# The experts of the second half and the closing stage in one block of the program

## The reference

```python
x = x + 0.5 * ffn(layernorm(x))
x = x + attention(layernorm(x))          # 16 heads of 8 features
x = x + 0.5 * ffn(layernorm(x))

def ffn(x):                               # 8 experts, 2 for each token, F = 176; shared F = 352
    scores = softmax(x @ gate_w.T)
    topk_w, topk_i = top_k(scores, 2)     # scaled to sum 2.5
    y = sum over the token's 2 experts of weight * ((silu(x @ w_gate[e]) * (x @ w_up[e])) @ w_down[e])
    return y + (silu(x @ sw_gate) * (x @ sw_up)) @ sw_down
```

## Time and profile before

| what | us |
|---|---|
| median of 3 runs | 1761.1 (1755.4 to 1765.99) |
| the profiled execution, its own time | 1749.63 |
| its span in the trace | 1747.9 |
| last matmul of own2 starts | 1681.49 |
| first matmul of finish starts | 1702.39 |
| last addition on DVE ends | 1745.34 |

### The profile page before, as it was taken

How to read it: one execution, slowest core, us unless ns; L and a number is a source line. 1 busy time by engine, 2 the same in 40 slices (tenths; PEclk the granted TensorE clock), 3 DMA queues, 4 the chain that set the end, 5 groups by cost and what they waited for, 6 DMA issues and landing times. The chain is left out here.

```text
span 1747.9 us, 26225 instructions
## 1 busy us (share of the span) xinstructions
PE 1422.1 (81%) x8158; PEld 796.4 (46%) x8158; DVE 1360.5 (78%) x2729; ACT 1102.3 (63%) x1688; POOL 947.2 (54%) x1040
## 2 busy tenths in 40 slices
PE   5788869996278999889988999888887795888846
PEld 3566647774123333333333333333325573666624
DVE  6777848885368888888888888888847784998938
ACT  6554447774047777777777777777667553766623
POOL 3676734223545554567744775544312673677765
PEclk9888989998569999999999999999998897999978
DMA  6411258784111100111111011111001114676727
GB/s 238 160 47 41 89 169 253 258 260 156 62 53 50 51 32 28 52 58 60 58 54 45 25 61 53 50 43 53 14 2 50 44 51 144 223 240 223 235 79 284
DMA packets 76459, 181.26 MB, mean 104 GB/s; under 512 B 19776, under 2 KB 21408, under 8 KB 76000
## 3 DMA queue, kind: packets, MB, share of 16 engines
q1 hardware_dynamic: 53408, 141.74, 24.4%
q0 software_dynamic: 21376, 37.03, 6.5%
q10 hardware_dynamic: 1536, 0.80, 0.2%
HBM read 105.03 MB, written 55.30 MB: 92 GB/s over the span
## 5 line engine op out<-in xcount | busy, mean ns | idle before, releaser
L2063 DVE TENSOR_REDUCE attn_neg_max<-attn_p_score 128x2 f32<-128x1024 f32 x512 | 623.4, 1222 | 122.7 <-PE attn_p_score L1718 118.2
L1869 ACT ACTIVATE attn_exps<-attn_p_score 128x1024 f32<-128x1024 f32 x512 | 521.7, 1025 | 218.2 <-PE attn_p_score L1704 215.7
L1718 PE MATMUL attn_p_score<-k_pack,q_pack 32*128 32x512 f32 x1024 | 262.2, 511 | 47.6 <-ACT attn_exps L1869 23.7
L1735 PE MATMUL attn_p_o<-attn_exps,values 128*32 128x512 f32 x2048 | 278.7, 616 | 8.6 <-ACT attn_o_raw L1875 3.3
L748 POOL DMA_INDIRECT rows<-send_rows,queue_slots x208 | 214.0, 1029 | 105.9 <-issue 60.3
L1704 PE MATMUL attn_p_score<-q_pack,k_pack 32*128 32x512 f32 x1024 | 255.7, 505 | 2.4 <-DVE attn_neg_max L2063 2.4
L1704 PEld LDWEIGHTS attn_p_score<-q_pack,k_pack 32*128 32x128 f32 x1024 | 95.2, 185 | 267.5 <-issue 236.0
L1362 POOL DMA_INDIRECT results<-own_y,own_to_row x156 | 155.9, 999 | 70.3 <-issue 44.2
L333 POOL DMA_INDIRECT attn_both<-results,queue_found_at x128 | 126.8, 991 | 44.1 <-issue 34.2
L1969 POOL DMA_DIRECT2D q_pack<-attn_max_rows x128 | 78.7, 617 | 124.5 <-ACT attn_max_rows L1863 120.1
L1718 PEld LDWEIGHTS attn_p_score<-k_pack,q_pack 32*128 32x128 f32 x1024 | 96.6, 187 | 97.7 <-ACT attn_exps L1869 72.9
(11 more groups left out here) (391 smaller groups left out, 3244.4 us busy)
## 6 DMA issues: line engine op xcount, KB each, us to landing
own_own<-own_weights SPq DMA_DIRECT2D x78, 640.0 KB, 4.4
own_rows<-rows SPq DMA_DIRECT2D x78, 264.0 KB, 3.3
results<-own_y SPq DMA_DIRECT2D x39, 256.0 KB, 4.7
q_pack<-attn_q_high SPq DMA_DIRECT2D x32, 256.0 KB
k_pack<-attn_k_high SPq DMA_DIRECT2D x32, 256.0 KB
sum_both<-results SPq DMA_DIRECT2D x16, 512.0 KB, 6.6
own_weights<-weights_pack SPq DMA_DIRECT2D x1, 5120.0 KB, 16.6
rows<-in_pad SPq DMA_DIRECT2D x16, 264.0 KB, 3.8
```

The costliest lines, as they stand in the source:

```text
L1718: last = nc.tensor.matmul(score_bank("max", b, n)[:, j % 2, :], pack["q"][b.par][rows, g, t * P:(t + 1) * P], pack["k"][b.par][rows, g, :] ...
L1735: last = nc.tensor.matmul(p_o[h * COLS:(h + 1) * COLS, :], values[b.par][:, t, g * QUAD + h, :], exps[(2 * u + h // 2) % len(exps)][:, h % ...
L1869: nc.scalar.activation(exps[n % len(exps)][:], score_bank("exp", b, n)[:], ACT.Exp, scale=inv_sqrt)\
L2063: V.tensor_reduce(neg_max[g % 2][:, j:j + 2, t], score_bank("max", b, n)[:], AX.X, ALU.max, negate=True).then_inc(max_read, 1)
```

## The change

`finish` goes away. Its work moves into a class `Closing`, whose methods are called at the end of each engine's list inside the block of `experts` own2. With it go these differences:

- There is no end of a block and no `cleanup_on_exit` between own2 and the closing work. PE goes on after its last `turn_y`, and needs only that DVE is through with two PSUM tensors (`gated_rest`, `xl_ready`).
- The wait for the scatters moves from POOL to SP, ahead of SP's first load of `both`. PE, ACT and DVE don't wait for them.
- The PSUM tensors for gate, up and down are those of own2, and one more (`p_y1`).
- The ring of `both` has 6 buffers, not 8, and SP starts with 6 loads.
- On DVE the results begin at n = 12 (`FIRST_SUM`), not n = 2: three lie in the last turns of the loop, 13 come after it.

```diff
+class Closing:
+    LAG, RING, FIRST_SUM = 2, 6, 12
...
+    def banks(self, p_x, p_gate, p_up, p_rest):
+        self.p_gate, self.p_up, self.p_y = p_x, [p_gate, p_up], [p_rest, self.p_y1]
+
+    def load(self, sp, i):
+        need(sp, self.added, i + 1 - self.RING)
+        sp.dma_start(self.both[i % self.RING][:], self.results[self.order[i]]).then_inc(self.loaded[i % self.RING], 16)
+
+    def transfers(self, sp):
+        for i in range(self.RING):
+            self.load(sp, i)
+        for i in range(NB):
+            if i + self.RING < NB:
+                self.load(sp, i + self.RING)
+            sp.wait_ge(self.out_ready, i + 1)
+            sp.dma_start(self.dst_b[self.order[i]], self.x_of(self.order[i])).then_inc(self.stored, 16)
+        sp.wait_ge(self.stored, 16 * NB)
...
+    def sums(self, pool):
+        for i in range(NB):
+            both = self.both[i % self.RING]
+            pool.wait_ge(self.loaded[i % self.RING], 16 * (i // self.RING + 1))
+            need(pool, self.out_ready, i - 1)
+            self.nc.gpsimd.tensor_tensor(self.total[i % 2][:], both[:, :, 0, :], both[:, :, 1, :], ALU.add)\
+                .then_inc(self.added, 1)
...
+            if n >= STILES + self.LAG and n % STILES == self.LAG:
+                self.add_shared(dve, n // STILES - 1)
+            if n >= self.FIRST_SUM:
+                self.result(dve, n - self.FIRST_SUM)
+        for i in range(self.tiles + self.LAG + 1 - self.FIRST_SUM, NB):
+            self.result(dve, i)
...
@@ experts, @block.sync
+            if closing:
+                for i in range(3):
+                    sp.wait_ge(sent[i], 16 * NT * len(range(i, NBLK, 3)))
+                closing.transfers(sp)
@@ experts, @block.tensor
+            if closing:
+                pe.wait_ge(gated_rest, NBLK)
+                pe.wait_ge(xl_ready, NBLK)
+                closing.products(pe)
@@ experts, @block.scalar
+            if closing:
+                closing.activations(act)
@@ experts, @block.gpsimd
-            if not in_place:
-                for i in range(3):
-                    pool.wait_ge(sent[i], 16 * NT * len(range(i, NBLK, 3)))
+            if closing:
+                closing.sums(pool)
@@ experts, @block.vector
+            if closing:
+                closing.additions(dve)
@@ program
         kept = Kept(nc, ctx)
-        with nc.cleanup_on_exit():
-            dispatch(nc, "send2", w, stream, queues[1], sent=sent, kept=kept)
-            experts(nc, "own2", w, queues[1])
-        finish(nc, "sum2", w, stream, queues[1], kept, y)
+        dispatch(nc, "send2", w, stream, queues[1], sent=sent, kept=kept)
+        closing = Closing(nc, ctx, "sum2", w, stream, queues[1], kept, y)
+        experts(nc, "own2", w, queues[1], closing=closing)
```

More of the change, by code:

```diff
@@ L1183, in __init__, with three, gate_up, down @@
         self.found_at = sb("found_at", [P, NPAIR, 2, NT2], U32)
-def experts(nc, name, w, queue, fills=(), in_place=False):
+class Closing:
+    LAG, RING, FIRST_SUM = 2, 6, 12
+    def __init__(self, nc, ctx, name, w, mid, queue, kept, dst):
+        self.nc, self.w, self.kept = nc, w, kept
+        sb = lambda n, shape, dt=F32: ctx.enter_context(nc.sbuf_tensor(f"{name}_{n}", shape, dt))
+        sem = lambda n: nc.alloc_semaphore(name=f"{name}_{n}")
+        ring = lambda make, n, count, *a: [make(f"{n}{i}", *a) for i in range(count)]
+        self.both, self.total = ring(sb, "both", self.RING, [P, NT, 2, D]), ring(sb, "total", 2, [P, NT, D])
+        self.silu, self.hidden = ring(sb, "silu", 2, [P, S]), ring(sb, "hidden", 2, [P, S])
+        self.hid_high, self.hid_low = ring(sb, "hid_high", 3, [P, S], F32R), ring(sb, "hid_low", 3, [P, S], F32R)
+        self.yt = sb("yt", [P, S])
+        self.p_y1 = ctx.enter_context(nc.psum_tensor(f"{name}_p_y1", [P, S], F32))
+        self.loaded, self.stored = ring(sem, "loaded", self.RING), sem("stored")
+        self.added, self.out_ready = sem("added"), sem("out_ready")
+        self.gate_ready, self.up_ready, self.silu_ready, self.gated_ready = (sem(n) for n in (
+            "gate_ready", "up_ready", "silu_ready", "gated_ready"))
+        self.high_ready, self.low_ready, self.down_done = sem("high_ready"), sem("low_ready"), sem("down_done")
+        self.y_copied, self.y_turned, self.mid_ready = sem("y_copied"), sem("y_turned"), sem("mid_ready")
+        self.results = queue.results[0:2 * NB * S, :].rearrange("(b p t c) d -> b p t c d", p=P, t=NT, c=2)
+        self.dst_b = dst.rearrange("(b p t) d -> b p t d", p=P, t=NT)
+        self.x_of = lambda k: mid[:, k * NT:(k + 1) * NT, :]
+        self.early = [k for k in range(NB) if k not in kept.BATCHES]
+        self.order = self.early + list(kept.BATCHES)
+        self.tiles = len(kept.BATCHES) * STILES
+    def banks(self, p_x, p_gate, p_up, p_rest):
[12 more added lines that the diff above has]
+        sp.wait_ge(self.stored, 16 * NB)
+    def three(self, out, weights, high, low, start, stop):
+        matmul = self.nc.tensor.matmul
+        matmul(out, weights[0], high, start=start, stop=False)
+        matmul(out, weights[1], high, start=False, stop=False)
+        return matmul(out, weights[0], low, start=False, stop=stop)
+    def gate_up(self, pe, n):
+        k, f = divmod(n, STILES)
+        m, cols = swidth(f), slice(f * P, f * P + swidth(f))
+        high, low = self.kept.high[k // 2][:, k % 2, :], self.kept.low[k // 2][:, k % 2, :]
+        need(pe, self.silu_ready, n - 1)
+        self.three(self.p_gate[n % 2][0:m, :], [a[:, cols] for a in self.w.gate], high, low, True, True)\
+            .then_inc(self.gate_ready, 1)
+        need(pe, self.gated_ready, n - 1)
+        self.three(self.p_up[n % 2][0:m, :], [a[:, cols] for a in self.w.up], high, low, True, True)\
+            .then_inc(self.up_ready, 1)
+    def down(self, pe, n):
+        k, f = divmod(n, STILES)
+        m = swidth(f)
+        pe.wait_ge(self.low_ready, n + 1)
+        if f == 0:
+            need(pe, self.mid_ready, k - 1)
+        self.three(self.p_y[k % 2][:], [a[0:m, f, :] for a in self.w.down], self.hid_high[n % 3][0:m, :],
+                   self.hid_low[n % 3][0:m, :], f == 0, f == STILES - 1).then_inc(self.down_done, 1)
+    def turn_y(self, pe, k):
+        pe.wait_ge(self.y_copied, k + 1)
+        for t in range(NT):
+            cols = slice(t * P, (t + 1) * P)
+            last = self.nc.tensor.transpose(self.p_y[k % 2][:, cols], self.yt[:, cols], self.w.ident[:])
+        last.then_inc(self.y_turned, 1)
+    def products(self, pe):
+        for n in range(self.tiles + self.LAG + 1):
+            if n < self.tiles:
+                self.gate_up(pe, n)
+            if 0 <= n - self.LAG < self.tiles:
+                self.down(pe, n - self.LAG)
+            if n >= STILES + self.LAG and n % STILES == self.LAG:
+                self.turn_y(pe, n // STILES - 1)
+    def activations(self, act):
+        activation = self.nc.scalar.activation
+        for n in range(self.tiles + self.LAG):
+            if n < self.tiles:
+                m = swidth(n % STILES)
+                act.wait_ge(self.gate_ready, n + 1)
+                need(act, self.gated_ready, n - 1)
+                activation(self.silu[n % 2][0:m, :], self.p_gate[n % 2][0:m, :], ACT.Silu).then_inc(self.silu_ready, 1)
+            if 0 <= n - 1 < self.tiles:
+                i, m = n - 1, swidth((n - 1) % STILES)
+                act.wait_ge(self.gated_ready, i + 1)
+                need(act, self.down_done, i - 2)
+                activation(self.hid_high[i % 3][0:m, :], self.hidden[i % 2][0:m, :], ACT.Copy).then_inc(self.high_ready, 1)
+            if n >= STILES + self.LAG - 1 and n % STILES == self.LAG - 1:
+                k = n // STILES - 1
+                act.wait_ge(self.down_done, (k + 1) * STILES)
+                need(act, self.y_turned, k)
+                activation(self.yt[:], self.p_y[k % 2][:], ACT.Copy).then_inc(self.y_copied, 1)
+    def sums(self, pool):
[5 more added lines that the diff above has]
+                .then_inc(self.added, 1)
+    def result(self, dve, i):
+        dve.wait_ge(self.added, i + 1)
+        if i >= len(self.early):
+            dve.wait_ge(self.mid_ready, i - len(self.early) + 1)
+        here = self.x_of(self.order[i])
+        self.nc.vector.tensor_tensor(here, self.total[i % 2][:], here, ALU.add).then_inc(self.out_ready, 1)
+    def add_shared(self, dve, k):
+        dve.wait_ge(self.y_turned, k + 1)
+        here = self.x_of(self.kept.BATCHES[k])
+        self.nc.vector.scalar_tensor_tensor(here, self.p_y[k % 2][:].rearrange("p (t d) -> p t d", d=D), 0.5, here,
+                                            ALU.mult, ALU.add).then_inc(self.mid_ready, 1)
+    def additions(self, dve):
+        V = self.nc.vector
+        for n in range(self.tiles + self.LAG + 1):
+            if n < self.tiles:
+                m = swidth(n % STILES)
+                dve.wait_ge(self.silu_ready, n + 1)
+                dve.wait_ge(self.up_ready, n + 1)
```

(40 more changed lines are left out.)

## The result

| | before | after |
|---|---|---|
| median, us (9 runs each) | 1757.5 (1751.11 to 1765.99) | 1747.32 (1738.47 to 1751.18) |
| span of the profiled execution | 1747.9 | 1748.5 |
| start of own2's last turn | 1681.49 | 1690.47 |
| from there to the end of the span | 66.4 | 58.0 |

The ratio is 0.9935 with a 95% interval from 0.9907 to 0.9963. Of 1757.5 us that is 11.4 us, or anything from 6.5 to 16.3; the two medians lie 10.2 us apart. The forecast was 7.8 us.

What follows compares the result with a forecast made beforehand. The end was taken to be bound by PE's 19.8 us wait before finish (14.5 scatters, 5.2 boundary). Starting 19.8 us earlier, less 12.0 us longer tiles and tail, gains 7.8 us: 1761.1 to 1753.3 us, range 1745 to 1761.

Steps and rivals of the forecast that it cites:

- PE's start: PE goes from own2's last turn straight into the closing tiles, at 1682.6, 19.8 us earlier than before.
- The tiles: Closing tiles on PE: tile 3 6.9 us after the first matmul, then 2.1 us a tile, tile 11 at 1707.2.
- POOL's sums 0 and 1: POOL's first two sums, amid the tiles, may each hold up one `sum_hid_low`: 0.7 us taken, bounds nothing and 1.2.
- Result 0: First result on DVE after the last tile's gate, up, down, turn and additions: ends at 1712.5.
- The tail: From result 0's end to result 15's: six pairs at 3.49 us, 0.1 more, and 3.95 us; 25.0 us in all.
- The close: After DVE's last result, the store and the close of the program take 2.56 us, as in the profile before.
- Sum: Start 19.8 us earlier, tiles and tail together 12.0 us longer: gain 7.8 us, median from 1761.1 to 1753.3 us.
- Rival B: In the tail sums and results alternate strictly, 27.6 us instead of 25.0; gain 5.2 us, 1756; chance 0.15.
- Rival C: The nine later loads bind the tail, costing 3.8 us; gain 4.0 us, 1757; chance 0.10.
- Rival D: Better start: sums hide (0.7 us) and PE has full clock without a slow stretch (1.8); gain 10.3, 1751; chance 0.15.
- E: PE's clock stays low through the closing tiles, 4.1 us each instead of 2.06; ten more cost 21 us, 1774; chance 0.03.
- F: Something holds the closing tiles until the scatters have landed, at 1697.1; 6.8 us slower, 1768; chance 0.02.

Runs made afterwards that it cites:

- the first experiment: The changed kernel, but PE waits for all scatters before the first closing tile; stretch from own2's last turn 73.6 us, ratio to the kernel before 1.004.

## Why the prediction was right

By its own steps, from the last turn of own2:

- PE's start: forecast 1.1 us after the last turn's start, measured 0.8. The slow clock came as forecast, 0.50 for 3.9 us.
- The tiles: from the first matmul to tile 3 it was 6.9 us, as forecast. From the last turn's start, tile 3 was forecast at 8.0 us and began at 7.7; tile 11 at 25.7 and at 25.2. The pace was 2.08 us for 2.1.
- POOL's sums 0 and 1: 0.7 us was the term that was mis-sized. One `sum_hid_low` took 0.3 us longer, and PE never waited for it; here the lower bound, nothing, was right. It depends on where the sums fall. With three sum buffers and the fast clock a `sum_hid_low` took 1.78 us beside POOL's first sum and PE waited 0.47 us, and the tiles lost 0.7 us:

```profile
1703.77 1.78 DVE L1326 TENSOR_TENSOR sum_hid_low<-sum_hidden,sum_hid_high 96x512 fp32r<-96x512 f32 x1
```

- Result 0 ends at 29.9 us (1.28 us is the row of results 0 and 1), forecast 31.0. The tail takes 54.9 - 29.9 = 25.0 us, forecast 25.0.
- The close: 3.1 us, forecast 2.56. In the waits of SP, the end of the block now waits 0.7 us for PE's sequencer, before 0.2.
- Sum: stretch 58.6 forecast, 58.0 measured; 8.4 us gained for 7.8. Result 0 came 1.1 us earlier than forecast and the close took 0.5 us more; that these partly cancel is luck.

The median of 1747.3 us is 6.0 us below the forecast 1753.3, near the lower end of its range. Of that, 3.6 us are the kernel before, whose median is 1757.5 over nine runs and was 1761.1 over three.

The split, taken from the two runs with PE's wait, was rougher than the sum. The late results cost 10.9 us for 12.0; the boundary alone is worth 3.7 us for 5.2 and the tiles beside the scatters 15.6 us for 14.5, so the overlap with the scatters is the main part.

Rival B falls: the seven pairs start 3.49 us apart. Two sums and two results with nothing overlapping, at 1.29 and 0.60 us, would be 3.8 us, as an estimate; a pair is 0.3 us shorter. The Trainium skill (SBUF — State Buffer, SBUF: two separate sides) says that a DVE operation with two SBUF inputs and a GpSimd operation that reads SBUF take a shared port pair as an exclusive lock, and the loser fully blocks. The trace agrees in the main, with the result of 1.73 us; the 0.3 us are what it differs by from the strict reading. The prediction saw the blocking in the 1.16 us ahead of result 14. That was the wait for its own sum; the blocking is in the length of the result's row.

Rival C is real, but one step further: at 1.745 us for each result six buffers cover the loads, at 1.2 us they don't. Rival D is what happened in its first half; its second half, a fast clock from the start, came in three of the other executions. The halves don't add up as D had it. In the run with three sum buffers the fast clock brought the tiles 1.9 us forward (D had 1.8), up to the `sum_hid_low` at 21.4 us, in the change 23.3. POOL's first sum then held this one up, and 1.2 us were left at result 0. E falls with a clock of 0.99 in the tiles. F, built as the first experiment, gave 7.2 us slower for a forecast of 6.8, and shows that the gain hangs on the missing wait. Of the chances, 0.55 stood on a change within 0.5% and 0.40 on faster by more. The ratio says 0.65%, in the second; its interval, 0.37 to 0.93%, and the 8.4 us of the trace (0.48%) leave open which it was.

## What to carry to other kernels

Ask of a wait at a stage's end who needs it. Here one queue's backlog (ten scatters that start after PE's last turn, landed 14.5 us behind it) held three engines that didn't depend on it, and moving the wait to the one consumer was worth 15.6 us. But the results that used to lie between the tiles went to the end, at a price of 10.9 us. The last rows of the old trace gave the length of the new tail, 25.0 us, to a tenth. After such a move look at the tail again: its next bounds, two engines in each other's way and then the transfers, were within 5 us.

## What the runs showed of the hardware

- PE's clock after the last block of own2 is not the same in each execution of nearly the same program: 0.50 or 1.00 in the first 4 us (once 0.62). The full clock brought the tiles 1.9 us forward and result 0 1.2 us.
- Two operations of 128x512 with both operands in SBUF, one on DVE and one on POOL, cost together 1.66 to 1.745 us where POOL alone takes 1.26 and DVE alone 0.60. A DVE operation that starts just after POOL's takes 1.73 us instead of 0.68. It is faster to give both to DVE: 1.20 us, as long as the loads keep up.
- Loads of 512 KB and stores of 256 KB together went at 411 GB/s where DVE waited for them, with each load 5.9 us from issue to landing in the median with four buffers, and 5.1 to 6.7 us with six.
- A block's end with its cleanup took 5.3 us of idle time ahead of the next load (6.60 us against 1.32 after the last scatter's end). The run that had only this out of the way was 3.7 us shorter in the stretch.
